# Where each engine reads two counts and four expert numbers into registers: after the last outer step, or inside it

## The chip, the cores and the metric
The kernel runs on one core of a Trainium2 chip. The metric is device time in microseconds of one execution, from many executions the median; lower is better. A profiled execution of the same program gives the rows below: its span runs from the first to the last instruction, and its own device time is a little longer than that span.

## What is computed
The input is x of 4 sequences x 512 tokens x 256 channels. It is layer-normalised (xn), and two branches run on xn:

```python
s = rwkv(xn)            # token shift, Wk, Wv, Wr; a scan over each sequence; Wo
probs = softmax(xn @ w_router.T)          # 16 experts
top_w, top_e = top_k(probs, 4); top_w /= sum(|top_w|)
for e in range(16):
    coeff = sum(where(top_e == e, top_w, 0))
    out += coeff * ((silu(xn @ w_gate[e]) * (xn @ w_up[e])) @ w_down[e])
x = x + s * silu(out)
```

2048 tokens with 4 experts each make 8192 rows of expert work.

## The kernel before
**Tiling.** The 8192 rows are sorted by expert, and each expert's rows are padded to whole tiles of 128. How many tiles there are is known only at run time: at least 64, at most 80. The kernel works on pairs of tiles. 32 pairs are always there (`NEED`), and up to 8 more stand in 4 optional blocks of two pairs each (`BLOCKS`). With the inputs profiled here 18 blocks of two pairs are in use, so 36 pairs: the 32, and two optional blocks (pairs 32 and 33, pairs 34 and 35).

**Counts.** VectorE writes into the small tile `used` how many blocks of two pairs there are (`used[0]`) and the number of pairs less 5 (`used[1]`, called `last`), and into `tile_expert` the expert of each tile. Both are complete before the outer steps begin.
**Order of the work.** The stretch in question is four outer steps of eight pairs, unrolled in the program, so o and u are constants and pair i is 8·o + u. Each engine has its own instruction stream, and they meet by semaphores. The order on each engine is written out by hand.
- POOL gathers the rows of pair i from memory (line 384) up to four pairs ahead, and scatters results of pair i - 6 (line 391). Each does two indirect DMAs.
- TensorE (`pair`, line 711): transposes x of pair i + 1 (line 683), reads the experts of pair i, multiplies tile 0 of pair i by gate and up (line 581, 4 matmuls), reads the experts of pair i - 2, multiplies pair i - 2 by down (8 matmuls), transposes the hidden rows of pair i - 1 (line 696), multiplies tile 1 of pair i by gate and up (4 matmuls).
- ScalarE copies transposed x out of PSUM (line 511), copies y of pair i - 2 (line 521), and computes silu of pair i (line 516). In the last outer step it also builds diagonal matrices (line 547).
- VectorE copies the transposed hidden rows of pair i - 1 (line 985), multiplies silu(gate) by up of pair i (`hidden`, line 990), and between these does pieces of the RWKV scan (lines 1003 to 1036).
- SyncE issues loads of finished slots of y, 2 MB each (line 296), once the scatters counted in `slot_done` have landed.

After the four outer steps every one of TensorE, ScalarE, VectorE and POOL calls `pairs_used`, and TensorE in addition reads the experts of the last two pairs of the run (`last_two`), which `down` uses after the optional blocks. Then `further_blocks` compares the count of blocks with a constant (a branch, line 245) and does the block or leaves.

**After the pairs** TensorE adds up y of the last tiles by matmuls with the diagonals (line 763), multiplies by Wo (line 581), and VectorE gates and adds the residual (lines 1084, 1090). The third 2 MB load waits until the rows of its slot have been scattered.

Of the kernel before, what the change touches and what calls it, by code (L numbers as in the profile page):

```python
# [16 lines left out]
OUTER = 4  # L17
# [11 lines left out]
def rwkv_times_moe(nc, x_in, vec_in, wkT_in, wvT_in, wrT_in, woT_in, wrouT_in, wg_in, wu_in, wd_in, out):  # L29
# [16 lines left out]
    with ctx:  # L46
# [3 lines left out]
        def sem(name):  # L50
            return ctx.enter_context(nc.semaphore(name))
# [20 lines left out]
        LAG = 6  # L72
# [138 lines left out]
        slots_known, weights_ready = sem("slots_known"), sem("weights_ready")  # L211
# [20 lines left out]
        def wait(eng, s, value):  # L232

            if not isinstance(value, int) or value > 0:
                eng.wait_ge(s, value)

        def pairs_used(eng):

            return (eng.value_load(used[0:1, 0:1], min_val=NEED // 2, max_val=NP // 2),
                    eng.value_load(used[0:1, 1:2], min_val=NEED - LAG + 1, max_val=NP - LAG + 1))  # L240
# [8 lines left out]
        def outer_steps(eng, step):  # L249

            for o in range(OUTER):
                step(o)
# [56 lines left out]
        def _(pool):  # L309
# [53 lines left out]
            def gather_indices(o, half):  # L363
                for b in range(XG):
                    if half == 1:
                        wait_alone(xg_in[b], 32 * (2 * o))
                    else:
                        wait_alone(xg_in[b], 32 * (2 * o - 1))
                pool.tensor_copy(g_idx[:, PAIRS * half:PAIRS * (half + 1)],
                                 tok_idx[:, bass.ds(2 * PAIRS * o + PAIRS * half, PAIRS)]).then_inc(gi_ready, 1)  # L370
                wait_alone(gi_ready, 2 * o + half)

            def scatter_indices(o, half):
                if not isinstance(o, int) or o > 0:
                    for par in range(2):
                        wait_alone(y_out[par], 16 * (PAIRS * o) if half == 1 else 16 * (PAIRS * o - PAIRS // 2))
                pool.tensor_copy(s_idx[:, PAIRS * half:PAIRS * (half + 1)],
                                 dst_idx[:, bass.ds(2 * PAIRS * o + PAIRS * half, PAIRS)]).then_inc(si_ready, 1)
                wait_alone(si_ready, 2 * o + half + 1)

            def gather(i, par, idx, n):
                wait_alone(xt_psum, i - XG + 1)
                for j in range(2):
                    pool.indirect_dma_start(out=xg[par][:, j, :], out_offset=None, in_=xn_rows,  # L384
                                            in_offset=bass.IndirectOffsetOnAxis(ap=idx[:, n + j:n + j + 1], axis=0)
                                            ).then_inc(xg_in[par], 16)
# [7 lines left out]

            last_row = pool.to_reg(ROWS - 1)

            def step(o):
                for u in range(PAIRS):
                    i = o * PAIRS + u
                    if u == 2:  # L400
                        gather_indices(o, 1)
                    if u == 6:
                        gather_indices(o + 1, 0)
                    if u == 2 and isinstance(o, int) and o == 0:
                        pool.wait_ge(proj_psum, BATCH * 3 * C)
                    gather(i, u % XG, tok_idx if isinstance(o, int) and o == 0 and u < XG else g_idx, 2 * u)
                    if u == 4:
                        if isinstance(o, int) and o == 0:
                            pool.wait_ge(dst_ready, 1)
                        scatter_indices(o, 0)  # L410
                    if u == 7:
                        scatter_indices(o, 1)
                    if u >= LAG:
                        scatter(i - LAG, u % 2, s_idx, 2 * (u - LAG))
                    elif not isinstance(o, int) or o > 0:
                        scatter(i - LAG, u % 2, s_idx, 2 * (u - LAG + PAIRS))

            outer_steps(pool, step)

            pool.wait_ge(slots_known, 3)  # L420
            blocks, last = pairs_used(pool)
            gather(NEED, NEED % XG, tok_idx, 2 * NEED)
            scatter(NEED - LAG, 0, dst_idx, 2 * (NEED - LAG))

# [12 lines left out]
        def _(act):  # L437
# [70 lines left out]
            def evac_x(i, par):  # L508
                act.wait_ge(xt_psum, i + 1)
                wait(act, gu_psum, i - 1)  # L510
                nc.scalar.copy(xTg[:, par].rearrange("p j c t -> p (j c t)"), ps[:, B_XT, :]).then_inc(xt_ready, 1)  # L511
# [11 lines left out]
            def step(o):  # L523
                first = isinstance(o, int) and o == 0
                for u in range(PAIRS):
                    i = o * PAIRS + u
                    evac_x(i + 1, (u + 1) % 2)
                    if u > 1 or not first:
                        evac_y(i - 2, u % 2, i - 2 - u % 2)
                    silu(i, u % 2)  # L530
                    if u % HALF == 1:
                        piece = o * C + u // HALF
                        act.wait_ge(args_ready, piece + 1)
                        nc.scalar.activation(args, args, ACT.Exp).then_inc(exps_ready, 1)  # L534
                    if isinstance(o, int) and o == OUTER - 1:
                        if u == 0:
                            act.wait_ge(weights_ready, 1)
                            act.wait_ge(wkv_ready, C * (OUTER - 1))
                        if u % HALF != 1:
                            diagonals(4)  # L540
# [3 lines left out]
            def diagonals(n):  # L544
# [3 lines left out]
                                         scale=coef4[:, 2 * BACK[0] + j, k:k + 1]).then_inc(diag_ready, 1)  # L548
                built[0] += n

            evac_x(0, 0)
            nc.scalar.activation(unmix[:, 0:1], unmix[:, 0:1], ACT.Silu)
            outer_steps(act, step)
            blocks, last = pairs_used(act)

            def more(k):
                for i in (NEED + 2 * k, NEED + 2 * k + 1):
# [19 lines left out]
        def _(pe):  # L577
# [130 lines left out]
            def experts_of(i):  # L708
                return [pe.value_load(tile_expert[0:1, bass.ds(2 * i + j, 1)], min_val=0, max_val=E - 1) for j in range(2)]

            def pair(i, u, first=None):
                par = u % 2

                if not first:
                    transpose_x(i + 1, (u + 1) % XG)
                now = first or experts_of(i)
                pe.wait_ge(xt_ready, i + 1)
                wait(pe, h_ready, i - 1)
                gate_up(par, 0, now[0])  # L720
                if first:
                    transpose_x(i + 1, (u + 1) % XG)
                    pe.wait_ge(proj_out, BATCH * 3 * C - 2)
                else:
                    if not isinstance(i, int) or i > 1:
                        down(i - 2, par, experts_of(i - 2))
                    transpose_h(i - 1, 1 - par)
                gate_up(par, 1, now[1]).then_inc(gu_psum, 1)

            def step(o):  # L730
                first = isinstance(o, int) and o == 0
                for u in range(PAIRS):
                    if first and u == 2:
                        pe.wait_ge(wdn_in, 16 * 2)
                    if first and u == 1:
                        pe.wait_ge(proj_out, BATCH * 3 * C)
                    pair(o * PAIRS + u, u, first_experts if first and u == 0 else None)

            pe.wait_ge(experts_ready, 1)
            first_experts = experts_of(0)  # L740
            transpose_x(0, 0)
            pe.wait_ge(wgu_in, 16 * 4)
            pe.wait_ge(proj_out, BATCH * 3 * C - 3)
            outer_steps(pe, step)
            blocks, last = pairs_used(pe)
            last_two = [experts_of(last + LAG - 3), experts_of(last + LAG - 2)]

            def more(k):
                for i in (NEED + 2 * k, NEED + 2 * k + 1):
# [45 lines left out]
        def _(dve):  # L795
# [191 lines left out]
            def hidden(i, par):  # L987
                dve.wait_ge(sg_ready, i + 1)
                wait(dve, ht_psum, i - 1)
                V.tensor_tensor(hid[:, par], sg[:, par], ps[:, B_G + 2 * par:B_G + 2 * par + 2, D:2 * D], ALU.mult).then_inc(h_ready, 1)  # L990
# [51 lines left out]
            def step(o):  # L1042
                first = isinstance(o, int) and o == 0
                for u in range(PAIRS):
                    i = o * PAIRS + u
                    if u > 0 or not first:
                        evac_h(i - 1, (u - 1) % 2)
                    for part in PARTS[u % HALF][0]:
                        wkv(o, u // HALF, part)
                    hidden(i, u % 2)  # L1050
                    for part in PARTS[u % HALF][1]:
                        wkv(o, u // HALF, part)

            outer_steps(dve, step)
            blocks, last = pairs_used(dve)

            def more(k):
                for i in (NEED + 2 * k, NEED + 2 * k + 1):
# [66 lines left out]
```

## Time and profile before
| | us |
|---|---|
| median of 3 runs | 334.74 |
| the three runs | 334.94, 334.74, 332.11 |
| profiled execution, device time | 335.54 |
| its span | 333.6 |

| engine | busy us | share of the span |
|---|---|---|
| TensorE matmul (PE) | 308.8 | 93% |
| TensorE weight load (PEld) | 189.5 | 57% |
| VectorE (DVE) | 260.0 | 78% |
| ScalarE (ACT) | 148.9 | 45% |
| GpSimd (POOL) | 205.6 | 62% |

### The profile page before, as it was taken

Reading aid. Unit: us, or ns where it says so; the run is one execution under the profiler, and the core shown is the slowest. Engines: PE = TensorE matmul, PEld = TensorE weight load, DVE = VectorE, ACT = ScalarE, POOL = GpSimd, SP = SyncE. Lnnn points to the kernel's source line nnn. Section 1 sums busy time; section 2 is a strip of 40 time slices with the busy share of each in tenths; the row PEclk is TensorE's granted clock in tenths of the full one; section 3 lists DMA queues with packets and bytes.
Section 4 is the critical chain, followed back from the end, with each engine's and each line's share of the span. In section 5 each row is a group of like instructions: output and inputs, shape, how many; then the busy total and the mean of one; then the engine's idle time right before and its main releaser. Section 6 shows DMA issues by size and latency. Waiting matters only on the chain.

```text
span 333.6 us, 4743 instructions
## 1 busy us (share of the span) xinstructions
PE 308.8 (93%) x1237; PEld 189.5 (57%) x1238; DVE 260.0 (78%) x522; ACT 148.9 (45%) x235; POOL 205.6 (62%) x210
## 2 busy tenths in 40 slices
PE   0899997998999999999999999999999969988894
PEld 0445443444666666666666666656666536667783
DVE  4788999489699699698698797896996951238893
ACT  1598763234722812822723624636656622220130
POOL 4400899757677777777778787777777732334000
PEclk9999999999999999999999999999999959999999
DMA  7799995313222224222234222134222292918743
GB/s 243 263 298 350 348 348 187 110 47 95 79 85 87 84 79 150 88 81 85 67 91 147 78 92 95 61 93 139 76 94 93 71 285 84 324 55 291 220 166 126
DMA packets 37864, 48.85 MB, mean 146 GB/s; under 512 B 3724, under 2 KB 33421, under 8 KB 37840
## 3 DMA queue, kind: packets, MB, share of 16 engines
q1 hardware_dynamic: 29600, 29.62, 27.7%
q0 software_dynamic: 7008, 18.10, 17.5%
q10 hardware_dynamic: 1232, 0.81, 0.8%
q8 instruction: 14, 0.23, 0.3%
q14 instruction: 10, 0.08, 0.1%
HBM read 35.94 MB, written 13.63 MB: 149 GB/s over the span
## 4 chain that ended last, share of the span: by engine, by line
PE 77%; DVE 11%; DMA 6%; issue 4%; ACT 1%; POOL 1%; DVEq 0%; POOLq 0%; SPq 0%
PE ps L581 63%; PE ps L683 5%; PE ps L696 4%; DVE ohB L961 4%; DVE arena L844 3%; DMA wbig<-y_rows 3%; PE ps L591 2%; DVE ohA L956 2%; PE ps L763 2%; DMA rT<-x_in 1%; DMA arena<-xn_rows,tok_idx 1%; DVE wbig L813 1%; DMA y_rows<-arena,e_idx 1%; POOL arena L384 0%; DVE wbig L890 0%
## 5 line engine op out<-in xcount | busy, mean ns | idle before, releaser
L581 PE MATMUL ps<-wbig,arena 128*128 x576 | 200.3, 491 | 3.3 <-ACT arena L511 1.7
L581 PEld LDWEIGHTS ps<-wbig,arena 128*128 128x128 f32 x576 | 104.7, 192 | 62.2 <-issue 56.4
L391 POOL DMA_INDIRECT y_rows<-arena,s_idx x52 | 64.6, 1242 | 20.3 <-issue 9.8
L384 POOL DMA_INDIRECT arena<-xn_rows,g_idx x56 | 56.5, 1009 | 16.8 <-issue 14.3
L521 ACT COPY arena<-ps 128x512 f32<-128x512 f32 x36 | 21.1, 586 | 73.8 <-PE ps L581 73.8
L581 PE MATMUL ps<-arena 128*128 128x512 f32 x96 | 43.9, 602 | 0.0
L516 ACT ACTIVATE arena<-ps 128x512 f32<-128x512 f32 x36 | 21.5, 597 | 46.2 <-PE ps L581 46.1
L348 POOL TENSOR_SCALAR ohB<-late 128x128 f16<-128x128 f32 x20 | 30.1, 1519 | 18.2 <-DVE late L895 18.2
L985 DVE COPY arena<-ps 128x512 f32<-128x512 f32 x36 | 24.8, 689 | 16.2 <-PE ps L696 15.4
L990 DVE TENSOR_TENSOR arena<-arena,ps 128x512 f32<-128x512 f32 x36 | 24.3, 674 | 12.7 <-ACT arena L516 12.1
L683 PEld LDWEIGHTS ps<-ident,arena 128*128 128x128 f32 x148 | 18.6, 143 | 23.2 <-issue 22.2
L581 PEld LDWEIGHTS ps<-arena 128*128 128x128 f32 x96 | 17.4, 190 | 17.7 <-issue 17.4
L683 PE MATMUL ps<-ident,arena 128*128 128x128 f32 x148 | 22.8, 277 | 3.1 <-issue 3.0
L384 POOL DMA_INDIRECT arena<-xn_rows,tok_idx x18 | 18.4, 1020 | 10.2 <-DVE tok_idx L972 5.0
L511 ACT COPY arena<-ps 128x512 f32<-128x512 f32 x37 | 21.3, 577 | 3.7 <-PE ps L683 3.6
L696 PE MATMUL ps<-ident,arena 128*128 128x128 f32 x144 | 21.6, 273 | 0.0
L1019 DVE TENSOR_TENSOR arena<-arena,vT 128x512 f32<-128x512 f32 x8 | 5.5, 693 | 20.3 <-ACT arena L534 20.3
L696 PEld LDWEIGHTS ps<-ident,arena 128*128 128x128 f32 x144 | 17.7, 141 | 4.3 <-issue 0.5
L391 POOL DMA_INDIRECT y_rows<-arena,e_idx x10 | 10.0, 996 | 16.0 <-ACT arena L521 14.4
L391 POOL DMA_INDIRECT y_rows<-arena,dst_idx x10 | 12.1, 1208 | 10.6 <-ACT arena L521 8.2
L844 DVE SCALAR_TENSOR_TENSOR arena<-arena,vec 128x512 f32<-128x512 f32 x24 | 16.9, 741 | 0.8 <-ACT arena L464 0.6
L464 ACT ACTIVATE arena<-arena,late 128x512 f32<-128x512 f32 x24 | 15.8, 714 | 0.0
(147 smaller groups left out, 380.9 us busy)
## 6 DMA issues: line engine op xcount, KB each, us to landing
wbig<-y_rows SPq DMA_DIRECT2D x3, 2048.0 KB, 9.4
wbig<-wg_in SPq DMA_DIRECT2D x2, 2048.0 KB, 13.1
wbig<-wu_in SPq DMA_DIRECT2D x2, 2048.0 KB, 18.9
wbig<-wd_in SPq DMA_DIRECT2D x2, 2048.0 KB, 12.9
rT<-x_in SPq DMA_DIRECT2D x4, 512.0 KB, 6.6
xn_rows<-rT SPq DMA_DIRECT2D x4, 512.0 KB, 3.5
kT<-x_in SPq DMA_DIRECT2D x8, 256.0 KB, 3.6
wbig<-y_rows SPq DMA_DIRECT2D x8, 256.0 KB, 4.1
```

Of the source, the lines that this page charges most:

```text
L348: ins = pool.tensor_scalar(ohB[:, t % RING, s], iota_row, prow[:, t, s:s + 1], val[:, 1 - s % 2, t:t + 1], ALU.is_equal, ALU.mult)
L384: pool.indirect_dma_start(out=xg[par][:, j, :], out_offset=None, in_=xn_rows, in_offset=bass.IndirectOffsetOnAxis(ap=idx[:, n + j:n + j + ...
L391: pool.indirect_dma_start(out=y_rows, in_=ysb[:, par, j, :], in_offset=None, out_offset=bass.IndirectOffsetOnAxis(ap=idx[:, n + j:n + j + ...
L511: nc.scalar.copy(xTg[:, par].rearrange("p j c t -> p (j c t)"), ps[:, B_XT, :]).then_inc(xt_ready, 1)
L516: nc.scalar.activation(sg[:, par], ps[:, B_G + 2 * par:B_G + 2 * par + 2, 0:D], ACT.Silu).then_inc(sg_ready, 1)
L521: nc.scalar.copy(ysb[:, par].rearrange("p j n -> p (j n)"), ps[:, B_Y, :]).then_inc(y_ready, 1)
L581: ins = nc.tensor.matmul(dst, lhsT(c), rhs(c), start=(c == 0), stop=(c == C - 1))
L683: ins = nc.tensor.transpose(ps[:, B_XT, (j * C + c) * P:(j * C + c + 1) * P], xg[b][:, j, c * P:(c + 1) * P], ident[:, :])
L696: ins = nc.tensor.transpose(ps[:, B_HT, (j * C + c) * P:(j * C + c + 1) * P], hid[:, par, j, c * P:(c + 1) * P], ident[:, :])
L844: ins = V.scalar_tensor_tensor(out=mix[b % 2][w][:, c, :], in0=xnT[:, c, b, 1:SEQ + 1], scalar=vec[:, (2 + w) * C + c:(2 + w) * C + c + 1] ...
L985: V.tensor_copy(hT[:, par].rearrange("p j c t -> p (j c t)"), ps[:, B_HT, :]).then_inc(ht_ready, 1)
L990: V.tensor_tensor(hid[:, par], sg[:, par], ps[:, B_G + 2 * par:B_G + 2 * par + 2, D:2 * D], ALU.mult).then_inc(h_ready, 1)
```

## The change
The reads move from behind the last outer step into it: on POOL before the gather of pair 27 (u = 3), on ScalarE after `evac_x` at u = 3, on VectorE after `hidden` at u = 3. On TensorE the two counts are read after pair 26 (u = 2), the experts of the run's last pair but one after pair 27 (u = 3) and those of its last pair after pair 28 (u = 4). What stands after the loop is the comparison alone. No read is added or removed.

```diff
@@ POOL @@
+            ends = []
             def step(o):
                 for u in range(PAIRS):
                     i = o * PAIRS + u
+                    if o == OUTER - 1 and u == 3:
+                        pool.wait_ge(slots_known, 3)
+                        ends.extend(pairs_used(pool))
...
-            pool.wait_ge(slots_known, 3)
-            blocks, last = pairs_used(pool)
+            blocks, last = ends
@@ ScalarE @@
                     evac_x(i + 1, (u + 1) % 2)
+                    if o == OUTER - 1 and u == 3:
+                        ends.extend(pairs_used(act))
...
-            blocks, last = pairs_used(act)
+            blocks, last = ends
@@ TensorE @@
                     pair(o * PAIRS + u, u, first_experts if first and u == 0 else None)
+                    if o == OUTER - 1 and u == 2:
+                        ends.extend(pairs_used(pe))
+                    if o == OUTER - 1 and u in (3, 4):
+                        last_two.append(experts_of(ends[1] + LAG - 6 + u))
...
+            ends, last_two = [], []
             outer_steps(pe, step)
-            blocks, last = pairs_used(pe)
-            last_two = [experts_of(last + LAG - 3), experts_of(last + LAG - 2)]
+            blocks, last = ends
@@ VectorE @@
                     hidden(i, u % 2)
+                    if o == OUTER - 1 and u == 3:
+                        ends.extend(pairs_used(dve))
                     for part in PARTS[u % HALF][1]:
                         wkv(o, u // HALF, part)
...
             outer_steps(dve, step)
-            blocks, last = pairs_used(dve)
+            blocks, last = ends
```

## Rows read from the trace of the kernel before

**Rows 1.** The chain of waits, 258 to 280 us: start, us, what.
```profile
258.65 1.72 PE ps L581 x4
...
264.69 1.72 PE ps L581 x4
266.41 3.00 issue
269.41 1.10 PE ps L683 x4
...
270.54 0.59 ACT arena L511
...
271.23 5.71 PE ps L581 x12
276.94 0.44 PE ps L696 x4
277.37 1.72 PE ps L581 x4
279.09 0.44 PE ps L683 x4
```
**Rows 2.** Stretches: PE, PEld, DVE, ACT, POOL busy, granted clock, DMA share, GB/s.
```profile
266.41:268.46 2.05, 0.00 (x0) 0.00 (x0) 2.05 (x3) 1.76 (x5) 1.44 (x3) 1.00 0.71 121
268.46:275.28 6.82, 5.14 (x10) 2.62 (x11) 3.39 (x4) 0.59 (x1) 1.86 (x2) 0.50 0.99 320
```
**Rows 3.** TensorE's sequencer by line: ns min/median/max, first and last start; 264 to 282 us.
```profile
L239 PEldq TENSOR_LOAD <-used x1: 306/306/306, 264.2 to 264.2; - x1
L709 PEldq TENSOR_LOAD <-tile_expert x4: 300/308/792, 265.7 to 268.5; - x4
L245 PEldq COMPARE_BRANCH  x2: 73/81/89, 269.2 to 280.8; - x2
```
**Rows 4.** TensorE's sequencer by line, between pairs 26 and 27.
```profile
L581 PEldq FUSED_REGOPS  x2: 46/46/46, 231.6 to 231.7; - x2
L235 PEldq EVENT_SEMAPHORE  x1: 51/51/51, 234.5 to 234.5; - x1
```
**Rows 5.** Pairs 27 and 28: VectorE's timeline, the sequencer by line, TensorE's timeline.
```profile
239.09 0.69 DVE L990 TENSOR_TENSOR arena<-arena,ps 128x512 f32<-128x512 f32 x1
L581 PEldq FUSED_REGOPS  x2: 46/46/46, 239.8 to 240.0; - x2
L581 PEldq FUSED_REGOPS  x2: 51/51/51, 241.6 to 241.7; - x2
242.53 3.61 PE L581 MATMUL ps<-wbig,arena 128*128 x12
```
**Rows 6.** Pair 29: the sequencer by line, TensorE's timeline.
```profile
L581 PEldq FUSED_REGOPS  x2: 51/51/51, 246.5 to 246.6; - x2
248.56 3.61 PE L581 MATMUL ps<-wbig,arena 128*128 x12
```
**Rows 7.** VectorE, ScalarE, POOL: their reads of the counts, timelines at u = 3.
```profile
L239 DVEq TENSOR_LOAD <-used x1: 550/550/550, 272.0 to 272.0; - x1
242.37 1.74 DVE L1031 RECIPROCAL arena<-arena 128x256 f32<-128x256 f32 x1
247.80 0.69 DVE L985 COPY arena<-ps 128x512 f32<-128x512 f32 x1
L239 ACTq TENSOR_LOAD <-used x1: 645/645/645, 266.5 to 266.5; - x1
240.13 0.58 ACT L521 COPY arena<-ps 128x512 f32<-128x512 f32 x1 [1.60 <-PE ps L581]
L239 POOLq TENSOR_LOAD <-used x1: 498/498/498, 241.8 to 241.8; - x1
211.12 1.56 POOL L391 DMA_INDIRECT y_rows<-arena,s_idx  x1 [0.80 <-ACT arena L521]
```
**Rows 8.** TensorE's timeline at the tail.
```profile
309.63 2.86 PE L763 MATMUL ps<-wbig,vT 128*128 128x256 f32 x12 [2.12 <-DMA wbig<-y_rows]
```

More of the change, by code:

```diff
@@ L549, in diagonals @@
                 built[0] += n
+            ends = []
             evac_x(0, 0)
@@ L1050, in step @@
                     hidden(i, u % 2)
+                    if o == OUTER - 1 and u == 3:
+                        ends.extend(pairs_used(dve))
                     for part in PARTS[u % HALF][1]:
                         wkv(o, u // HALF, part)
+            ends = []
             outer_steps(dve, step)
-            blocks, last = pairs_used(dve)
+            blocks, last = ends
             def more(k):
```

## The prediction
> **What bounds the kernel now.** I start with the shares of the page: TensorE is busy 93% of the span. Then the chain of waits in order of time around the end of the outer steps [rows 1]. It is made of TensorE's own matmuls; one pair takes 264.69 - 258.65 = 6.04 us, and in it TensorE waits for nobody. At 266.41 comes the one long hole before the tail: 3.00 us of "issue", that is, no other engine is waited for. The same point of the next pair is reached at 277.37, so this pair took 12.68 us, 6.64 more than its neighbours.
>
> The stretches [rows 2] say what the rest of the 6.64 is. TensorE was idle from 266.41, at 268.46 its granted clock fell from 1.00 to 0.50 (2.4 to 1.2 GHz), and it stayed there for 6.8 us. So the 6.64 are 3.00 of hole, 0.66 because four transposes took 1.10 and not 0.44 as at 279.09, 0.7 of standing bare for ScalarE's copy (0.59 and the hand-over), and the rest, 2.3, because the next 12 matmuls ran at 1.2 GHz (5.71 us, where such a group otherwise takes 3.4 to 3.6 [rows 5]).
>
> The sequencer's rows [rows 3] fill the hole. It began the two counts at 264.2, the four expert reads ran from 265.7, the branch stands at 269.2, and the transposes start 0.2 after it. That is 5.0 us of reads, of which 2.2 lie beside matmuls that had been handed over before. The comparison is cheap: 73 to 89 ns, and the one at 280.8, with no reads ahead of it, leaves no hole in the chain.
>
> **What the change removes on TensorE.** All six reads go from that place. The sequencer then stands at the branch at 264.3, 2.1 us before the queued matmuls run out, and the transposes for pair 33 follow without a hole; their input was copied by ScalarE long before. Without the hole I let the clock stay at 2.4 GHz. Gain: 6.64 us.
>
> **What it adds on TensorE**, three times a delay of the sequencer, which costs only what exceeds its lead over the array.
> - *The two counts after pair 26.* Price 265.5 - 264.2 = 1.3 us [rows 3] (the first expert address stands 0.1 before the first expert read). The sequencer was through with pair 26 at 231.7 and its next event is at 234.5 [rows 4]: 2.8 us in which it waits for ScalarE's copy, late behind an Exp. The reads fit in. Cost 0. Bounds: 0, and 1.3 if the lead is not there.
> - *Two expert reads after pair 27.* Four reads took 269.2 - 265.6 = 3.6 us, one of them 0.5 longer than the others (792 ns against 300 [rows 3]); so two take about 1.6. Here the sequencer has no slack from waiting: it gets past pair 27 at 240.0, just after VectorE's `hidden` ended (239.09 + 0.69 = 239.78) [rows 5], and goes straight on to pair 28's own reads. The address for pair 28's first gate and up comes at 241.6, a matmul can follow about 0.1 later (in rows 1 the copy that was waited for ends at 271.13, the matmul starts at 271.23), and the matmul is due at 242.53. Lead 0.8, delay 1.6: TensorE stands for 0.8. The next point, the address of `down`, then comes just when it is due, with nothing more to pay. Cost 0.8. Bounds: 0, and the full 1.6.
> - *Two expert reads after pair 28.* Address of pair 29 at 246.5, matmul due at 248.56 [rows 6]: lead 1.9 with the 0.1. Both sequencer and array come 0.8 later by the stall before, so 1.9 stands against 1.6. Cost 0. Bounds: 0, and 1.6; with 0.3 to spare it is the thinnest cover of the three.
>
> The short lead at pair 27 comes from a semaphore: nothing behind gate and up's second half can be issued before `hidden` is done, and `hidden` ends 2.75 us before the matmul that is due. The Trainium skill ("TensorE: Matmul & The Clock Gate", the paragraph on engine queue depths) gives TensorE a queue of 64 instructions, more than one whole pair of matmuls and weight loads here. If that queue were what sets the lead, all three groups would be hidden and the sum would be 6.64. This trace shows a lead of 0.8, so the sum goes by the rows.
>
> **The other engines** [rows 7]. VectorE's two reads (550 ns the first; with the second and the register work behind each about 1.5 us) stand between `hidden` and the second reciprocal of pair 27. `hidden` is handed over while the first reciprocal (1.74 us from 242.37) still runs, so they lie beside these two. Fully bare they would put the next copy from 247.8 to 249.3, and `down` needs it only 1.7 us after 248.56. Cost 0; cover: the 1.7 us and the first reciprocal. ScalarE's reads (645 ns the first, some 1.8 for both) run beside four diagonal copies and `evac_x`; the next instruction is at 240.13 after 1.60 of idleness. Cost 0. On POOL the wait for `slots_known` has long been met; the reads (498 ns, 1.3 for both) lie beside the two scatters from 211.12 on (pair 20's), behind which the gather of pair 27 is queued; gathers are four pairs ahead. Cost 0. SyncE's queue is not touched. At the end VectorE also loses its 1.5 us from 272.0 on. There it was not late, since TensorE was; with TensorE on time they would have used up most of the slack before pair 31's `down`, and that they go keeps the 6.64 whole.
>
> **What is late next.** Nothing new, I think: from 277 on all was anchored to TensorE, the third 2 MB load too, so the tail moves as a block.
>
> **Sum.** 6.64 - 0.8 = 5.84. The profiled execution: 335.54 - 5.84 = 329.7 (span 333.6 to 327.8). It lies 0.8 over the median; 334.74 - 5.84 = 328.9. The run of 332.11 is 2.7 under the others, which is about what the low clock cost (0.66 + 2.3 = 2.9); if that is a run in which the clock did not fall, it gives 332.11 - (6.64 - 2.9 - 0.8) = 329.2. I take 329.0. With the bounds: 328.1 if no read shows, 334.74 - 6.64 + 4.5 = 332.6 if all three groups do.
>
> **The rivals.**
> - *The clock falls elsewhere.* TensorE waits 2.12 us for the third load at the tail [rows 8], as long as it was idle before the clock fell at 268.46. There it stayed at full clock in this execution. If it falls there once things have moved, the sum by diagonals and Wo run at 1.2 GHz: 2.9 as before, 329.0 + 2.9 = 331.9. For it: the equal length. Against: it didn't in the profile, and no run shown is longer by that much. 10%.
> - *The moved reads stand bare.* The lead of the sequencer is smaller than I read it: 330.5 to 332.6. 7%.
> - *The hole has a second cause.* The DMA share is 0.71 and then 0.99 just there [rows 2], a 2 MB load, and one read took 792 ns. If fetches or the gathers are held up by it, TensorE would stall there anyhow for most of the 3.0, and lose its clock: 334 to 335. Against: the reads fill the hole to 0.2 us. 4%.
> - *The reads are not moved in effect*, because the order within the stream stays: 334.7. 1%.
> - *Slower: the lead is never regained.* After pair 27 the sequencer is 1.6 late, and if each of the eight pairs 28 to 35 pays that again, the cost is 12.8: 334.74 - 6.64 + 12.8 = 340.9. It decides from 0.83 per pair (6.64 / 8). Against: a pair's own four reads and addresses are about 4 us of sequencer time in 6.04, so 2 us per pair are there to catch up. 3%.
>
> **How the numbers follow.** My case 75%: 328.0 to 330.2. Range 327.9 to 332.0: my case, the tail clock and most of the bare reads, some 85 to 90% by count, and less because I may be wrong about a median of few runs. A difference under 1% (3.3 us) is about what a measurement can't tell from none. Faster by over 1% (under 331.4): my case and half of the bare reads and a remainder for runs with a late clock fall in a minority, 0.81. Within 1%: tail clock, second cause, no effect, 0.15. Slower 0.04.
>
> **What would show it.** In the chain no "issue" near 266, the x12 group behind it at about 3.45 us, granted clock 1.00 throughout; six TENSOR_LOADs of TensorE at 231.8, 240.1 and 245.5 or so; a hole of 0.8 ahead of pair 28's first gate and up near 242.5 and none ahead of pair 29's; VectorE, ScalarE and POOL without new idleness at u = 3; the tail's wait still about 2.1. Wrong would be: a hole at 266 without reads, a granted clock of 0.50 anywhere, a stall over 1.6 at pair 28, or stalls that repeat in pairs 29 to 31.

## The result, and the profile after

| | before | after |
|---|---|---|
| median, 4 runs each | 334.84 us | 329.81 us |
| lowest and highest | 332.11, 335.87 | 329.19, 330.01 |
| ratio, with its 95% interval | | 0.9869 [0.982, 0.9919] |
| profiled execution, device time | 335.54 | 329.84 |
| its span | 333.6 | 328.1 |

The forecast was 329.0, in a range of 327.9 to 332.0. In the changed kernel the matmul line 581 is line 588, 683 is 690, 696 is 703, 709 is 716, 763 is 774; on ScalarE 511 is 515, 521 is 525; on VectorE 985 is 996, 990 is 1001.

The chain of waits of the kernel after, the stretch that answers to [rows 1] (start, us, what):

```profile
260.01 1.72 PE ps L588 x4
...
266.05 1.72 PE ps L588 x4
267.77 0.44 PE ps L690 x4
268.20 3.44 PE ps L588 x12
...
272.09 1.72 PE ps L588 x4
```

The hole is gone: the same point comes after 272.09 - 266.05 = 6.04 us, where it took 12.68. The same chain some 25 us earlier, from pair 27's second gate and up on:

```profile
240.79 1.72 PE ps L588 x4
242.51 0.44 PE ps L690 x4
242.95 0.72 issue
243.67 3.83 PE ps L588 x12
247.50 0.44 PE ps L703 x4
247.93 1.72 PE ps L588 x4
...
250.09 3.44 PE ps L588 x12
```

Here is what the change costs: 247.93 - 240.79 = 7.14 and not 6.04, so 1.10 us, and the group of pair 29, from 250.09, has its usual 3.44: nothing more. 6.64 - 1.10 = 5.54, and the spans differ by 5.5. That the two agree so closely is in part luck: the outer steps start 0.3 later here (`hidden` of pair 0 at 81.08, in the kernel before at 80.76), and the third 2 MB load takes 0.3 less (9.10 and 9.37 in the chains). Busy time by stretch (us, then PE, PEld, DVE, ACT, POOL, granted clock, DMA share, GB/s), against [rows 2]:

```profile
266.00:276.00 10.00, 10.00 (x38) 5.82 (x37) 8.52 (x10) 4.12 (x10) 6.96 (x8) 1.00 0.95 256
```

The DMA engines are busy at 0.95 from 266 to 276, with the 2 MB load in them as before, beside a TensorE that is busy all the time at full clock. This execution has one low clock, at 54.6 to 58.0, behind a wait of 1.9 for POOL's one-hot tiles. That is one of the prediction's signs of being wrong ("a granted clock of 0.50 anywhere"). It lies long before the places of the change and says nothing on the hole, but it isn't free: the eight matmuls behind it take 5.21 us in the chain, in the run `whole` below, without it, 3.51. The sequencer's rows of TensorE, by line (ns min/median/max, first and last start), which answer to [rows 3 to 6]:

```profile
L239 PEldq TENSOR_LOAD <-used x1: 303/303/303, 232.1 to 232.1; - x1
L235 PEldq EVENT_SEMAPHORE  x1: 51/51/51, 234.8 to 234.8; - x1
L588 PEldq FUSED_REGOPS  x2: 46/46/46, 240.1 to 240.2; - x2
L716 PEldq TENSOR_LOAD <-tile_expert x2: 304/308/312, 240.5 to 241.4; - x2
L588 PEldq FUSED_REGOPS  x2: 51/51/51, 243.6 to 243.7; - x2
L588 PEldq FUSED_REGOPS  x2: 51/51/51, 249.4 to 249.6; - x2
L245 PEldq COMPARE_BRANCH  x2: 73/81/89, 265.7 to 275.5; - x2
```

The counts are read from 232.1 and the sequencer still waits until 234.8. The experts are read from 240.5, and the address of pair 28's first gate and up slips from 1.6 after the end of pair 27's addresses [rows 5] to 3.4 after it. The comparison stands at 265.7, while pair 31's last matmuls are still queued.

### The profile page after: what moved, and what is told of

It is laid out like the page before. It is cut to its first block, busy times and chain, and to the rows that moved or that the text cites. A ratio compares the mean times of both kernels' runs of the same rounds, so it can differ in the third digit from the quotient of the medians.

```text
span 328.1 us, 4743 instructions
## 1 busy us (share of the span) xinstructions
PE 306.5 (93%) x1237; PEld 188.5 (57%) x1238; DVE 260.2 (79%) x522; ACT 148.9 (45%) x235; POOL 204.1 (62%) x210
## 4 chain that ended last, share of the span: by engine, by line
PE 83%; POOL 6%; DMA 5%; DVE 3%; issue 1%; ACT 1%; DVEq 0%; SPq 0%; POOLq 0%
PE ps L588 69%; POOL ohB L348 6%; PE ps L690 5%; PE ps L703 5%; DMA wbig<-y_rows 3%; PE ps L598 2%; PE ps L774 2%; DMA rT<-x_in 1%; DVE wbig L824 1%; DMA y_rows<-arena,e_idx 1%; DVE wbig L901 0%; PE ps L646 0%; PE ps L614 0%; PE ps L669 0%; DVE wbig L827 0%
## 5 line engine op out<-in xcount | busy, mean ns | idle before, releaser
L588 PEld LDWEIGHTS ps<-wbig,arena 128*128 128x128 f32 x576 | 103.6, 190 | 61.2 <-issue 55.3
L588 PE MATMUL ps<-arena 128*128 128x512 f32 x96 | 45.6, 621 | 0.0
L598 PE MATMUL ps<-ident,rT 128*128 128x128 f32 x32 | 6.6, 356 | 9.4 <-ACT rT L451 9.4
```

Of the source, the lines that this page charges most:

```text
L588: ins = nc.tensor.matmul(dst, lhsT(c), rhs(c), start=(c == 0), stop=(c == C - 1))
```

## The experiments

All ratios are to the kernel before on the same chip. Chips differ by as much as many of the effects here: the kernel before has a median of 335.6 us on the chip of the first four rows, 336.1 on that of the next four and 339.1 on that of the last four. So only ratios, or times within one group of four, are compared. `end5` and `double_u3` were executed once each, so they are read by their traces and not by their times.

| kernel | ratio to before, 95% interval | us |
|---|---|---|
| whole (the change) | 0.9862 [0.9813, 0.9911] | 330.25 |
| pe_only | 0.9862 [0.9811, 0.9912] | 330.18 |
| spread | 0.9802 [0.9752, 0.9852] | 328.38 |
| others_only | 0.9992 [0.9946, 1.0038] | 334.90 |
| hidden_first | 0.9781 [0.9715, 0.9847] | 328.80 |
| counts_only | 0.9878 [0.9839, 0.9918] | 332.25 |
| end5, one execution | | 331.33 |
| double_u3, one execution | | 334.53 |
| whole_again | 0.9854 [0.9809, 0.9899] | 333.52 |
| spread_again | 0.9763 [0.9715, 0.9811] | 331.34 |
| spread_tail | 0.9685 [0.9645, 0.9726] | 328.39 |
| before_tail | 0.9838 [0.9781, 0.9895] | 334.82 |

**The theory:** only TensorE's reads were on the path; a group of reads costs what exceeds the lead that the sequencer has over the array at its place. **The rivals:** the other engines' reads, the branch or the 2 MB load made the hole; or the gain is how executions fall, with the clock.

### The change as a whole, once more

> The changed kernel again, as the measure for the three beside it on this chip. By my theory the profile shows one new hole, ahead of pair 28's first gate and up (about 0.9 us plus 0.2 for refilling), and none at the end of the outer steps: span 327.5 to 328.3, 5.5 us under the kernel before. If the gain hangs on how the execution happens to fall, its runs should spread over 3 us as those of the kernel before do.

Its span is 327.1, with the one hole of 0.72 ahead of pair 28. Its six times lie between 329.07 and 330.86, those of the kernel before between 333.27 and 339.55 (337.29 without the three longest of seventeen). So the hole is where the theory has it and is the only one; its 0.72 counts from the modelled end of the matmul before, and by the starts of the instructions it is 0.88 (item 4 under "Why the prediction was right"). The span is 0.4 under the expected range.

### One part alone: which engine's reads were on the path
```diff
 # pe_only: POOL, ScalarE, VectorE read behind the loop
-                        ends.extend(pairs_used(pool))   # and act, dve
...
+            blocks, last = pairs_used(pool)             # and act, dve
 # others_only: TensorE reads behind the loop
-                        ends.extend(pairs_used(pe))
-                        last_two.append(experts_of(ends[1] + LAG - 6 + u))
...
+            blocks, last = pairs_used(pe)
+            last_two = [experts_of(last + LAG - 3), experts_of(last + LAG - 2)]
```

> TensorE's reads are moved as in the change; POOL, ScalarE and VectorE read at the end as before. Theory (only TensorE's reads were on the path): the same as the changed kernel to 0.3 us, 5.0 to 5.5 under before; VectorE's reads after pair 31's scan end at about 273.7 on the changed kernel's time, its copy at 274.4, and down of pair 31 is due at 276.0. Rival (VectorE's reads become the next wait there): a hole of up to 1.5 us in pair 33 and a time 0.5 to 1.5 above the changed kernel.

> POOL, ScalarE and VectorE read inside the last outer step as in the change; TensorE reads all six at the end as before. Theory: no gain, within 0.3 us of the kernel before, with the hole of 3.0 us and the low granted clock at 266 to 275 as before. Rival (the other engines' reads delayed the first optional pair too): up to 1.5 us faster than before.

pe_only has the whole gain (0.9862, the same as the change on the same chip), others_only none (0.9992). The chain of waits of others_only has the hole where it was:

```profile
263.75 1.72 PE ps L588 x4
265.46 2.55 issue
268.02 0.64 PE ps L690 x4
...
269.61 5.40 PE ps L588 x12
```
```profile
L716 PEldq TENSOR_LOAD <-tile_expert x4: 300/308/343, 264.7 to 267.1; - x4
```

The hole is 2.55 us and not 3.00. The second fence says why: none of the four expert reads took longer than 343 ns, where the kernel before had one of 792 [rows 3]. So some 0.45 of the 3.00 was one slow read. before_tail lies between, with a slowest read of 506 ns and a hole of 2.85. In others_only the low clock follows too, but for 3.4 us (270.3 to 273.7), and the pair takes 11.70 us where it took 12.68. What makes a read slow isn't shown; the 2 MB load isn't needed for it, since TensorE has single reads of 0.43 to 0.69 us in each outer step of the kernel after, before the first such load is issued at 265.9.

The chain of waits of pe_only, at pair 33, shows all that VectorE's reads at the end cost once TensorE is on time: an x12 group of 3.63 us where the one before took 3.45, so 0.2, and no hole.

```profile
267.38 3.45 PE ps L584 x12
...
273.42 3.63 PE ps L584 x12
```

### The same reads at other places
```diff
 # spread
-                    if o == OUTER - 1 and u == 2:
+                    if o == OUTER - 2 and u == 6:
                         ends.extend(pairs_used(pe))
-                    if o == OUTER - 1 and u in (3, 4):
-                        last_two.append(experts_of(ends[1] + LAG - 6 + u))
+                    if o == OUTER - 1 and u in (2, 6):
+                        last_two.append(experts_of(ends[1] + LAG - 3 + u // 6))
```

> The changed kernel, but TensorE's six reads stand at the three places of a pair where its sequencer waits 2.8 us for ScalarE's copy behind the Exp: counts after pair 22, experts after pair 26 and after pair 30. Theory (each group costs what exceeds the sequencer's lead at its place): no hole at pair 28, the 1.1 us come back, 328.7 where the changed kernel has 329.8, span about 327.0. Rival (a read costs TensorE about the same wherever it stands, or the hole at pair 28 has another cause than the reads): no difference from the changed kernel.

> The spread kernel a second time, beside the changed one on the same chip. Theory: 1.1 us under the changed kernel in executions of equal clock; medians 0.8 to 1.8 apart. Rival (the difference seen before was how executions fell): none.

No hole at pair 28 nor anywhere up to the tail. The timeline of TensorE in spread (start, us, engine, line, operation):

```profile
239.71 1.88 PE L588 MATMUL ps<-wbig,arena 128*128 x4
241.43 0.60 PE L690 MATMUL ps<-ident,arena 128*128 128x128 f32 x4
241.87 3.61 PE L588 MATMUL ps<-wbig,arena 128*128 x12
...
245.75 1.88 PE L588 MATMUL ps<-wbig,arena 128*128 x4
```

6.04 us per pair again. Within each of the two groups spread is below the change: 328.38 against 330.25, and 331.34 against 333.52. The medians are 1.9 and 2.2 apart (0.8 to 1.8 was expected), where the hole accounts for 1.1; the intervals of the ratios overlap, so the traces, not the medians, carry this verdict, and the rest of the difference stays open. The granted clock may be part of it: the profiled execution of whole_again has a mean clock of 0.999 and took 330.83 us, its other five 0.987 to 0.993 and 333.2 to 335.7, while spread_again lies mostly at 0.993 to 0.999.

### What sets the lead at pair 27
```diff
 # hidden_first: hidden of u = 2 and 6 ahead of part 4 of the scan
-            PARTS = (((0,), (1, 2)), ((), (3,)), ((4,), (5, 6)), ((7,), (8, 9)))
+            PARTS = (((0,), (1, 2)), ((), (3,)), ((), (4, 5, 6)), ((7,), (8, 9)))
```

> The changed kernel with its reads where it has them, but VectorE does `hidden` of every pair with u = 2 and 6 ahead of part 4 of the scan and not behind it (PARTS), in all outer steps; the result of each operation is the same. So `hidden` of pair 26 ends some 2 us earlier. Theory (TensorE's sequencer gets its lead at pair 27 from the end of `hidden`, the semaphore ahead of gate and up's second half): its lead grows from 0.8 to over 1.6, the hole ahead of pair 28 goes, 1.1 us under the changed kernel. Rival (the queue to the array is full there, or the reads themselves can't run beside matmuls): the hole of 0.7 stays.

VectorE's timeline, the sequencer's addresses of pair 27's second half and of pair 28's first, and TensorE's timeline in hidden_first:

```profile
237.16 0.69 DVE L1001 TENSOR_TENSOR arena<-arena,ps 128x512 f32<-128x512 f32 x1 [0.19 <-ACT arena L520]
```
```profile
L588 PEldq FUSED_REGOPS  x2: 46/46/46, 238.6 to 238.8; - x2
L588 PEldq FUSED_REGOPS  x2: 51/51/51, 242.1 to 242.2; - x2
```
```profile
240.59 1.88 PE L588 MATMUL ps<-wbig,arena 128*128 x4
242.31 0.60 PE L690 MATMUL ps<-ident,arena 128*128 128x128 f32 x4
242.75 3.61 PE L588 MATMUL ps<-wbig,arena 128*128 x12
...
246.63 1.88 PE L588 MATMUL ps<-wbig,arena 128*128 x4
```

The reads stand where the change has them, `hidden` of pair 26 starts at 237.16 (239.35 in the change), the sequencer goes on at 238.6 and not at 240.1, and the hole is gone. The sequencer gains 1.5 of the 2.2, because by then its own reads and addresses for pair 27 fill the time up to 238.8. So the semaphore of `hidden` set the lead, not a full queue; the reads themselves run beside matmuls without cost. (The change wasn't measured on this chip, so the expected 1.1 us between the medians isn't tested here.)

### The size of the cost: more reads at pair 27, fewer or other reads at the end
```diff
 # double_u3
                     if o == OUTER - 1 and u in (3, 4):
+                        if u == 3:
+                            experts_of(ends[1] + LAG - 3)
                         last_two.append(experts_of(ends[1] + LAG - 6 + u))
 # counts_only: the change, without the expert reads in the loop
+            last_two = [experts_of(last + LAG - 3), experts_of(last + LAG - 2)]
 # end5: spread, and behind the loop
+            for _ in range(5):
+                pe.value_load(used[0:1, 0:1], min_val=NEED // 2, max_val=NP // 2)
```

> The changed kernel with the two expert reads after pair 27 made twice, the second time for nothing. Theory (each group costs what exceeds the lead): the hole ahead of pair 28 grows by the whole price of two reads, 1.5 to 1.6, from 0.7 to 2.3; there is no lead left to take it, also the transposes of pair 29 come late. Span 1.6 above the changed kernel's, 2.9 more if the clock falls behind it. Rival (the hole has another cause): 0.7 as before.

> The changed kernel, but TensorE reads the four experts at the end, behind the last outer step; the two counts stay after pair 26. Theory: the hole at the end is the reads less the lead, so 3.0 - 1.3 = 1.7 us, then 0.7 for ScalarE's copy. If the granted clock stays at 1.00 behind the shorter hole: 6.64 - 2.4 = 4.2 under the kernel before, 331.3 on its chip; if it falls as before, 1.3 under it. Rival (the branch or the 2 MB load makes the hole, not the reads): 3.0 as before.

> The kernel with the reads spread over the three places of long lead, and five further reads of a count, whose values nobody uses, by TensorE behind the last outer step, where the kernel before had its six. Theory: 5 x 0.65 = 3.25 us of reads against a lead of 2.1 with the branch: a hole of 1.2 to 1.4 at the end, 0.7 more for the copy, about 2 us above the spread kernel, granted clock mostly kept. Rival (a hole there comes only with reads whose values the branch or the next pairs need): none.

TensorE's timeline in double_u3:

```profile
239.59 1.88 PE L588 MATMUL ps<-wbig,arena 128*128 x4
242.39 0.63 PE L690 MATMUL ps<-ident,arena 128*128 128x128 f32 x4 [0.92 <-issue]
244.01 3.74 PE L588 MATMUL ps<-wbig,arena 128*128 x12 [0.99 <-DVE arena L1003]
...
248.02 1.45 PE L588 MATMUL ps<-wbig,arena 128*128 x3
```

The stall stands in two holes, ahead of the transposes and ahead of the matmuls, and the pair takes 248.02 - 239.59 = 8.43: 2.39 above 6.04, against 1.10 in the change. The second pair of reads costs 1.3, its whole price: 2 x 0.65, as for the counts, where I had put down 1.5 to 1.6. The row at 244.01 names VectorE's `hidden` (L1003) as what ended the wait. That is `hidden` of pair 27, which ended at 243.88; but of VectorE's work the kernel makes the first of these matmuls wait only for `hidden` of pair 26, which ended at 239.00, and in the change they start at 243.67, ahead of `hidden` of pair 27 at 244.29. The sequencer's reads fill the time: the last is done at 243.74, the address stands at 243.90.

The chains of counts_only and end5 at the end of the outer steps:

```profile
263.96 1.72 PE ps L588 x4
265.68 1.37 issue
267.05 0.64 PE ps L690 x4
...
268.68 3.71 PE ps L588 x12
...
272.82 1.72 PE ps L588 x4
```
```profile
263.33 1.72 PE ps L588 x4
265.05 1.41 issue
...
272.19 1.72 PE ps L588 x4
```

Four expert reads, or five reads whose values nobody uses, make nearly the same hole, and the pair takes 8.86 in both, 2.8 above its neighbours and not 6.64. The predicted holes were 1.7 and 1.2 to 1.4. The branch and the 2 MB load are there as in the change and in spread, which have no hole at this place, so they make none by themselves. The granted clock stayed at 1.00 behind both holes; in counts_only 3.8 of the 6.64 come back though only 1.3 us of reads are gone. Its median agrees: 3.9 us under the kernel before, though its profiled execution has a low clock at the tail instead, as the next part shows.

### The tail
In others_only, spread, spread_again, hidden_first, counts_only and double_u3 the profiled execution has a granted clock of 0.50 that begins at the end of TensorE's wait for the third 2 MB load, or up to 0.65 us ahead of that end (double_u3) or 0.4 behind it (spread_again). In before, after, whole, whole_again, pe_only and end5 it has none there, and none in spread_tail and before_tail, whose order is another. The stretches of spread:

```profile
300.20:302.34 2.14, 0.02 (x2) 0.02 (x1) 0.00 (x0) 0.00 (x0) 0.00 (x0) 1.00 0.65 232
302.34:305.75 3.41, 3.41 (x8) 2.78 (x9) 3.38 (x9) 0.00 (x0) 0.00 (x0) 0.50 0.50 163
```
```profile
302.32 4.54 PE L774 MATMUL ps<-wbig,vT 128*128 128x256 f32 x12 [2.12 <-DMA wbig<-y_rows]
```

This was my first rival, and it is real. None of the three profiles of the changed kernel has it, but that doesn't settle how often it falls there: most executions of `whole` have a mean clock of 0.992 to 0.994 and 330.1 to 330.9 us, where the profiled one has 0.997 and 329.07, and where the clock was low in them isn't recorded. It can be taken away:

```diff
 # spread_tail, before_tail
             for k in range(TOPK - 1):
+                if k == TOPK - 2:
+                    for n in FRONT:
+                        rwkv_out(n)
                 pe.wait_ge(y_in[k], 16)
                 for n in BACK:
                     slot_rows(n, k)
-            for n in FRONT:
-                rwkv_out(n)
```

> The spread kernel, and at the tail TensorE does the product with Wo of the first ten tiles ahead of the wait for the third 2 MB load, not behind it. Theory (the granted clock falls in that wait of 2.1 us in some executions, and the wait is on the path): no wait there, granted clock 1.00 to the end in each profile, 2 to 3 us under the spread kernel, and its runs lie closer together; VectorE's own chain at the tail becomes the bound, which keeps it from being more. Rival (the tail is bound by VectorE and the loads already): no difference but the rarer slow clock, under 1 us.

> The kernel before with the tail's order alone changed as in spread_tail. Theory: 2 to 3 us under before, 332 to 333; the hole at 266 and the clock behind it are as they were, so what the moved reads give and what the tail gives add up, and spread_tail is lower by 6 to 7. Rival (both repair one and the same low clock): spread_tail lower than this by less than 4.

> The changed kernel a third time: 0.986 of before, 329 to 331 us, hole of 0.7 ahead of pair 28. By theory any granted clock under 1.00 late in its profile lies behind the wait for the third load, none behind the hole at pair 28, which is shorter than 1 us.

TensorE's timeline at the tail of spread_tail, against [rows 8]:

```profile
297.09 5.34 PE L774 MATMUL ps<-wbig,vT 128*128 128x256 f32 x24
302.27 8.80 PE L588 MATMUL ps<-woT,rT 128*128 128x256 f32 x40
310.90 3.94 PE L774 MATMUL ps<-wbig,vT 128*128 128x256 f32 x16
314.67 1.89 PE L588 MATMUL ps<-woT,rT 128*128 128x256 f32 x8
```

The wait is gone, the clock is 1.00 up to the end of TensorE's work, and the six times lie between 327.94 and 328.80, those of spread_again between 329.96 and 332.02 with one at 335.63. The median is 2.95 us under that of spread_again, as expected (2 to 3), and in the chain of waits VectorE's own work bounds the tail from 305.8 on. spread_tail is the fastest kernel here, 0.9685 of before, where the change has 0.9854 on the same chip; these intervals don't touch. before_tail has 0.9838 with a hole of 2.85 and the low clock, at 271.5 to 278.3, in place: 4.3 us under the kernel before, where I had expected 2 to 3. spread_tail is 6.4 under before_tail (expected 6 to 7; the rival said less than 4), so the two repairs are not one and the same. They don't add up in full, though: spread_tail is spread with the new tail, and 0.9838 x 0.9763 would be 0.960, where it has 0.9685. The new order gives 4.3 us on the kernel before and 2.95 on spread; intervals of half a per cent each way can't tell whether the difference is real. whole_again has its hole of 0.72, and its profiled execution a full clock throughout; its median of 333.52 lies over the expected 329 to 331, but its ratio of 0.9854 is the expected 0.986: this chip is slower for all kernels.

## Why the prediction was right

1. *The hole was the six reads, not the comparison.* Shown: it goes with TensorE's reads alone (pe_only), stays without them (others_only), and any reads in that place bring it back by their number (counts_only, end5). Some 0.45 of the 3.00 was a single slow read (others_only), which is the grain of truth in the rival of the second cause.
2. *With the hole goes the low clock, 6.64 us in all.* Shown in the trace after (12.68 to 6.04 us) and in counts_only and end5, where a hole of 1.4 left the clock up. The 6.64 is the loss of the profiled execution. On the chip of the first four rows, eight of the seventeen executions of the kernel before have a mean clock of 0.993 or 0.994 and took 333.3 to 334.3 us, only 3 to 4 over the changed kernel; in those the low clock was shorter than in the profiled one, where the mean is 0.989; where it lay no trace shows. The prediction had reckoned with that case, from the run of 332.11, and came to nearly the same time.
3. *Counts after pair 26: cost 0.* Right; read at 232.1, the wait for ScalarE's copy lasted to 234.8.
4. *Experts after pair 27: cost 0.8.* The mechanism was right and is shown by hidden_first, spread and double_u3; the size was 1.10. The times here are starts of single instructions, which lie 0.16 ahead of those in the chain. The reads took 240.35 to 242.03, so 1.7 and not 1.6. The transposes started at 242.35 and the first matmul behind them, due 0.44 later at 242.79, started at 243.67: 0.88. The other 0.22 is what I had left out: the group from there to the next transposes took 3.66 and not 3.44, 0.1 at the first matmul behind the hole and 0.1 at `down`, whose address came just too late.
5. *Experts after pair 28: cost 0.* Right, with 0.4 to spare: address at 249.4, matmul at 249.93.
6. *The other engines: cost 0, and VectorE's move needed to keep the 6.64 whole.* The first half is right: others_only is level with before, and VectorE's pieces around pair 27 keep their spacing. The second is worth 0.2 us, in pe_only.
7. *Sum.* 5.84 forecast, 5.54 in the chain. That the median came out at 329.81 and not 329.0 is 0.3 of this; the rest lies within what executions differ by. The gain in the medians is 5.03 us, 1.5%.
8. *The rivals.* The stall does not repeat in pairs 29 to 35 (the slower case). The low clock at the tail is real in single executions, and my 10% for it was too low as a statement on executions: 6 of the 12 profiles with the old order of the tail have it. It cost about 1.7 in the matmuls behind it in spread (4.54 us for 12 that take 2.86), less than the 2.9 that I had put; in double_u3, where it lasted 6.8 us, it cost 3.1 (5.49 for the 12, and 9.25 where the next 40 take 8.80). Had it fallen in full in most executions, the median would have come out near 331.9; that it came out at 329.81 is on this point luck and not reasoning.

## What to carry to other kernels

Here a register read by an engine's sequencer cost nothing while the engine had queued work longer than the read, and its full price beyond (with 0.2 us more where the array had run dry); so count the lead at each place, from the address computation to the matmul that is due, and put reads where the sequencer waits for another engine anyway. Here a semaphore wait and not the length of the queue set that lead, and moving what it waits for was as good as moving the read. A hole on TensorE can cost more than twice its length once the clock falls behind it (3.00 us cost 6.64), so a hole that is only shortened can already return most of it, and work that is ready belongs into the wait that is left.

## What the runs showed of the hardware beyond that

- The clock does not follow from the length of one hole alone. After holes of 3.00, 2.85 and 2.55 us at the end of the outer steps it was 0.50 (before, before_tail, others_only), after 1.37 and 1.41 it was not (counts_only, end5). But at the tail a wait of 2.12 us left it at 1.00 in the kernel before and brought it to 0.50 in spread, one of 3.07 left it in end5 and brought it down in double_u3, and early in the program one of 1.88 brought it down in after and one of 1.86 left it in spread_again. The low clock lasted 6.8 us in some (before, before_tail, double_u3) and 3.4 in others. What decides stays open; one to three profiles of a kernel can't tell it.
- The time of an execution goes with its mean granted clock. On the chip of the first four rows the kernel before took 333.3 to 334.3 us at 0.993 and 0.994, and 336.4 to 337.3 at 0.982 and 0.983. So the clock is at least part of why the kernel before spreads over 4 us there, even without its three longest executions, and spread_tail over 0.9.
- The kernel before had medians from 334.8 to 339.1 us on different chips. All four profiles from the slowest chip lose 1.8 to 1.9 us in one place: from `hidden` of pair 0 to that of pair 5 they take 31.1 to 31.2 us, the other profiles 29.2 to 29.3. Why is open.
